# Other slots in the run-out for the gate steps and expert groups of the last three tiles

## The reference, cut to what matters

```python
x = x + 0.5 * ffn(layernorm(x))          # job b
x = x + attention(layernorm(x))          # 16 heads, scores below the 31st largest masked
x = x + 0.5 * ffn(layernorm(x))          # job a

def ffn(h):                              # 16 experts of width 64
    logits = normalize(h) @ normalize(sim) - sigmoid(gates)
    rw = softmax(where(mask, relu(logits), -inf))   # mask: logits > 0, else the top 2
    q, k, v = (sum_e rw[e] * (h @ proj[e]) for proj in (q_proj, k_proj, v_proj))
    att = softmax(causal(q @ k.T / 8)) @ v
    return sum_e (rw[e] * att) @ o_proj[e]
```

## Time and profile before

| | |
|---|---|
| median of 3 runs | 4722.92 us (4720.09 to 4724.39) |
| the profiled execution | 4726.93 us |
| its span in the profile | 4725.1 us |
| mean granted clock of TensorE | 0.933 |
| busy: TensorE, its weight loads | 87%, 72% |
| busy: VectorE, ScalarE, POOL | 93%, 84%, 63% |

### The profile page before, as it was taken

How to read it: one execution, slowest core, us unless ns; L and a number is a source line. 1 busy time by engine, 2 the same in 40 slices (tenths; PEclk the granted TensorE clock), 3 DMA queues, 4 the chain that set the end, 5 groups by cost and what they waited for, 6 DMA issues and landing times. The chain is left out here.

```text
span 4725.1 us, 123794 instructions
## 1 busy us (share of the span) xinstructions
PE 4132.2 (87%) x33100; PEld 3423.4 (72%) x33100; DVE 4393.5 (93%) x10203; ACT 3967.9 (84%) x10181; POOL 2995.0 (63%) x4946
## 2 busy tenths in 40 slices
PE   6778899899999889999998999998899989987777
PEld 5556777777777777777777777777777777765555
DVE  2499999999999999999999999999999999999982
ACT  2488889898898889989888998988899889888772
POOL 1445677677667767766776776677677667654440
PEclk8889999999999999999999999999999999988888
DMA  3111111121111111111111111111111111111011
GB/s 100 45 27 35 49 50 53 50 55 50 52 51 51 53 50 55 50 52 51 51 53 50 55 50 52 51 51 53 50 53 50 54 51 51 51 38 26 22 30 50
DMA packets 244162, 232.66 MB, mean 49 GB/s; under 512 B 27123, under 2 KB 176628, under 8 KB 243316
## 3 DMA queue, kind: packets, MB, share of 16 engines
q1 hardware_dynamic: 243444, 224.49, 16.6%
HBM read 214.98 MB, written 9.44 MB: 47 GB/s over the span
## 5 line engine op out<-in xcount | busy, mean ns | idle before, releaser
L1027 DVE MAX8 M<-W 128x8 f32<-128x512 f32 x2688 | 1735.2, 681 | 57.8 <-DVE W L1029 2.5
L679 PE MATMUL pQ<-wf_sb,HS 128*128 128x192 f32 x8192 | 1545.3, 345 | 81.3 <-POOL HS L419 54.1
L679 PEld LDWEIGHTS pQ<-wf_sb,HS 128*128 128x128 f32 x8192 | 1438.3, 203 | 129.5 <-issue 65.9
L1029 DVE MATCH_REPLACE8 W<-M,W 128x512 f32<-128x512 f32 x1664 | 1115.0, 676 | 0.0
L1072 POOL TENSOR_TENSOR XL<-S,LM 128x512 f32<-128x512 f32 x384 | 445.6, 1160 | 908.4 <-ACT LM L909 895.5
L698 PE MATMUL pST<-ident,S 128*128 128x128 f32 x4096 | 747.9, 283 | 15.4 <-ACT S L897 15.4
L924 ACT ACTIVATE OUT<-S,M 128x512 bf16<-128x512 f32 x1024 | 741.5, 724 | 0.0
L928 ACT ACTIVATE S<-S,M 128x512 f32<-128x512 f32 x1024 | 737.2, 720 | 0.0
L700 PE MATMUL pST<-steep,OUT 128*128 128x128 bf16 x4096 | 731.8, 222 | 0.0
L1029 DVE MATCH_REPLACE8 W<-M,S 128x512 f32<-128x512 f32 x1024 | 684.3, 676 | 0.0
L1027 DVE MAX8 M<-S 128x8 f32<-128x512 f32 x1024 | 651.5, 678 | 20.8 <-ACT S L897 10.7
(11 more groups left out here) (267 smaller groups left out, 6585.2 us busy)
## 6 DMA issues: line engine op xcount, KB each, us to landing
RB<-rows_b SPq DMA_DIRECT2D x384, 256.0 KB, 3.3
RB<-rows_a SPq DMA_DIRECT2D x384, 256.0 KB, 3.3
x_b<-in_x SPq DMA_DIRECT2D x64, 128.0 KB, 2.8
out_y<-y SPq DMA_DIRECT2D x64, 128.0 KB, 1.8
wf_sb<-in_wf SPq DMA_DIRECT2D x4, 768.0 KB, 7.4
rows_b<-rwT_b SPq DMA_DIRECT2D x64, 8.0 KB, 1.3
wof_sb<-in_wof SPq DMA_DIRECT2D x1, 1024.0 KB, 7.1
rows_a<-rwT_a SPq DMA_DIRECT2D x64, 8.0 KB, 1.4
```

The source lines that it names most:

```text
L679: mm = nc.tensor.matmul(pQ[:, 0:QKV], HS[:, k % 2, e, i, :], wf_sb[:, i, at:at + QKV], start=k + e + i == 0, stop=(k, e, i) == (3, 3, 1))
L1027: nc.vector.max(m, src[i]).then_inc(s_tk, 1)
L1029: nc.vector.match_replace(W[:, i, :], m, src[i], -BIG).then_inc(s_tk, 1)
```

## The change

For the last three tiles of job a, a second table `QUICK` gives the gate steps and the four expert groups other slots. Relative to the tile, `shift` to `rw_st` were at slots 50 to 61 and are at 49 to 53, right behind `lg` at 49. `hs` was at 64, 66, 68, 70 and is at 60, 63, 67, 70. The next tile's gate steps, at 65 to 69 on this tile's count, so meet its groups, and its first two groups stand among the small products of the tile before.

The counts of events (`FILLS`, `CHUNKS`) follow the new slots. Three more edits go beyond the last tiles or beside them: `ctx_norm` is no longer moved to VectorE for tiles 62 and 63; `rw_st` waits for the `RB2` load of two tiles before in place of its `mix`, in all tiles; the scaling of `wof` comes 16 slots later in the run-in. `QUICK` has slots for job b too, but its `ENDS` is empty.

```diff
-        "gate_exp": 88, "gate_em": 89, "gate_sum": 90, "rw": 91, "rwT": 92, "rw_st": 93, "hs": 96, "qkv": 104,
+        "gate_exp": 88, "gate_em": 89, "gate_sum": 90, "rw": 91, "rwT": 92, "rw_st": 93, "hs0": 96, "hs1": 98, "hs2": 100, "hs3": 102, "qkv": 104,
...
+ENDS = {"a": range(TILES - 3, TILES), "b": range(0)}
+QUICK = {
+    "a": {k: v - 2 * TILE for k, v in {
+        "shift": 81, "top": 82, "pair": 82, "repl": 83, "gate": 83, "gate_exp": 84, "gate_em": 84, "gate_sum": 85,
+        "rw": 85, "rwT": 85, "rw_st": 85, "hs0": 92, "hs1": 95, "hs2": 99, "hs3": 102}.items()},
...
+def slot_of(n, key, t):
+
+    return (QUICK[n] if t in ENDS[n] and key in QUICK[n] else AT[n])[key] + t * TILE
+
+
+def events(n, key):
+
+    if key not in QUICK[n]:
+        return [(AT[n][key], TILE, TILES)]
+    others = [t for t in range(TILES) if t not in ENDS[n]]
+    return [(slot_of(n, key, others[0]), TILE, len(others))] + [(slot_of(n, key, t), SPAN, 1) for t in ENDS[n]]

...
-CHUNKS = {(n, c): (AT[n]["hs"] + 2 * c, TILE, TILES) for n in "ab" for c in range(4)}
+CHUNKS = [[ev for n in "ab" for ev in events(n, f"hs{k}")] for k in range(4)]
...
-            return due(w, j + ahead, J.at[key], TILE, TILES) if key in J.at else None
+            if key in QUICK[J.n] and w.lo == w.hi:
+                for t in ENDS[J.n]:
+                    if SPAN * w.lo + j + ahead == slot_of(J.n, key, t):
+                        return t, t - TPB * w.lo
+            at = due(w, j + ahead, J.at[key], TILE, TILES) if key in J.at else None
+            return None if at and key in QUICK[J.n] and w.lo == w.hi and at[0] in ENDS[J.n] else at
+
+        def apart(J, t, key, other, back=0):
+
+            if isinstance(t, int):
+                return slot_of(J.n, other, t - back) - slot_of(J.n, key, t)
+            return J.at[other] - J.at[key] - back * TILE
 
         def chunk_no(w, j):
-            return earlier(w, j, CHUNKS.values())
+            return earlier(w, j, sum(CHUNKS, []))
 
...
-            if not isinstance(t, int) or key in ("x_rstd", "h_rinv", "y_rstd"):
+            if not isinstance(t, int) or key in ("x_rstd", "h_rinv", "y_rstd", "ctx_norm"):
                 return False
             if J.n == "b":
                 return t < TPB
-            return t >= TILES - (3 if key in ("hs", "sc_nmax", "sc_rec", "mix") else 2)
+            return t >= TILES - (3 if key[:2] == "hs" or key in ("sc_nmax", "sc_rec", "mix") else 2)
 
...
-                    held(sp, q["read"], fill(J.n, w, j + J.at["rwT"] - J.at["rw_st"]) + 1)
+                    held(sp, q["read"], fill(J.n, w, j + apart(J, t, "rw_st", "rwT")) + 1)
                     if not (isinstance(t, int) and t < 2):
-                        held(sp, s_mix, earlier(w, j + J.at["mix"] - J.at["rw_st"] - 2 * TILE, MIXES.values()) + 1)
+                        held(sp, s_rb2, 32 * earlier(w, j + apart(J, t, "rw_st", "mix", 2), MIXES.values()) + 32)
...
-                    if at := tile(J, "hs", w, j, 3 - 2 * k):
+                    if at := tile(J, f"hs{k}", w, j, 3):
...
-                if (w.lo, j) == divmod(AT["b"]["hs"], SPAN):
+                if (w.lo, j) == divmod(AT["b"]["qkv"] + 8, SPAN):
```

More of the change, by code:

```diff
@@ L67 @@
         "lg": -41, "shift": -40, "top": -39, "pair": -38, "repl": -37, "gate": -34, "gate_exp": -33,
-        "gate_em": -32, "gate_sum": -31, "rw": -30, "rwT": -29, "rw_st": -28, "hs": -24, "qkv": -16, "qkT": -15,
+        "gate_em": -32, "gate_sum": -31, "rw": -30, "rwT": -29, "rw_st": -28, "hs0": -24, "hs1": -22, "hs2": -20, "hs3": -18, "qkv": -16, "qkT": -15,
         "sc": -14, "sc_max": -13, "sc_nmax": -11, "sc_exp": -10, "sc_rec": -9, "sc_norm": -8, "pT": -6,
@@ L72 @@
 }
+ENDS = {"a": range(TILES - 3, TILES), "b": range(0)}
[3 more added lines that the diff above has]
+        "rw": 85, "rwT": 85, "rw_st": 85, "hs0": 92, "hs1": 95, "hs2": 99, "hs3": 102}.items()},
+    "b": {k: v - SPAN for k, v in {
+        "shift": -41, "top": -40, "pair": -40, "repl": -39, "gate": -39, "gate_exp": -38, "gate_em": -38,
+        "gate_sum": -37, "rw": -37, "rwT": -35, "rw_st": -35, "hs0": -30, "hs1": -27, "hs2": -22,
+        "hs3": -19}.items()},
+}
+def slot_of(n, key, t):
[5 more added lines that the diff above has]
+    return [(slot_of(n, key, others[0]), TILE, len(others))] + [(slot_of(n, key, t), SPAN, 1) for t in ENDS[n]]
 PROJ = {"Q0": 57 - SPAN, "K0": 59 - SPAN, "V0": 61 - SPAN, "V1": 62 - SPAN, "Q1": 68 - SPAN, "K1": 70 - SPAN}
@@ L78 @@
 FILLS = {
-    "a": {k: (AT["a"][k], TILE, TILES) for k in ("ctxT", "x", "hT", "lg", "rwT", "qkT", "sc", "pT", "attT", "y")},
-    "b": {k: (AT["b"][k], TILE, TILES) for k in ("hT", "lg", "rwT", "qkT", "sc", "pT", "attT", "y", "xn")}
-    | {k: (s, SPAN, NB) for k, s in PROJ.items()},
+    "a": [ev for k in ("ctxT", "x", "hT", "lg", "rwT", "qkT", "sc", "pT", "attT", "y") for ev in events("a", k)],
+    "b": [ev for k in ("hT", "lg", "rwT", "qkT", "sc", "pT", "attT", "y", "xn") for ev in events("b", k)]
+    + [(s, SPAN, NB) for s in PROJ.values()],
 }
-CHUNKS = {(n, c): (AT[n]["hs"] + 2 * c, TILE, TILES) for n in "ab" for c in range(4)}
+CHUNKS = [[ev for n in "ab" for ev in events(n, f"hs{k}")] for k in range(4)]
 GROUPED = {n: (AT[n]["qkv"], TILE, TILES) for n in "ab"}
@@ L162, in fill @@
 def fill(n, w, j):
-    return earlier(w, j, FILLS[n].values())
+    return earlier(w, j, FILLS[n])
 def build(nc, x, wqk, bqk, wv, bv, wo, bo, sim, gates, wf, wof, out):
@@ L378, in layer @@
                 t, c = at
-                eng.wait_ge(q["read"], fill(J.n, w, j + J.at["lg"] - J.at["shift"]) + 1)
+                eng.wait_ge(q["read"], fill(J.n, w, j + apart(J, t, "shift", "lg")) + 1)
                 ns.tensor_tensor(J.L[:], J.Lr[:], sig[:], ALU.subtract).then_inc(q["shift"], 1)
@@ L410, in layer @@
             for k in range(4):
-                if at := mine("hs", -2 * k):
+                if at := mine(f"hs{k}"):
                     t, c = at
                     m = chunk_no(w, j)
-                    chunks = [ev for key, ev in CHUNKS.items() if key[1] % 2 == k % 2]
+                    chunks = CHUNKS[k % 2] + CHUNKS[k % 2 + 2]
                     eng.wait_ge(s_rb[k % 2], 16 * earlier(w, j, chunks) + 16)
@@ L668, in group @@
                 for k in range(4):
-                    if at := tile(J, "hs", w, j, -1 - 2 * k):
+                    if at := tile(J, f"hs{k}", w, j, -1):
                         t, c = at
@@ L810, in leave @@
                     if not (isinstance(t, int) and t < 2):
-                        act.wait_ge(s_hs, chunk_no(w, j + J.at["hs"] + 6 - J.at["hT"] - 2 * TILE) + 1)
+                        act.wait_ge(s_hs, chunk_no(w, j + apart(J, t, "hT", "hs3", 2)) + 1)
                     act.wait_ge(q["full"], n)
```

## The result

The changed kernel takes 4733.01 us (median of 13 runs, 4731.04 to 4734.31) against 4723.02 (13 runs, 4718.32 to 4724.64) for the kernel before in the same rounds: ratio 1.0021, 95% interval 1.0014 to 1.0028. It is 10 us, 0.2%, slower. The forecast was 4725.5, with 0.72 on a change within 0.2% (9.4 us) and 0.10 on slower; 10.0 us lies just outside those 0.2%, and the time lies on the upper end of the range, where rival C stood.

A forecast was written before the change was run, and what follows sets the result against it. VectorE was taken to set the pace until its last search, so the change could pay only after it, perhaps in the run-in; order +0.1 and clock +2.5 us, +2.6 on the median 4722.92, gave 4725.5 us, range 4711 to 4733.

The forecast's parts named there:

- rival C: Low clock takes group 3 of tiles 60 to 62 and the y matmuls behind: +8.7 to +12, 4731.7 to 4735; chance 0.12.
- The bound: VectorE sets the pace of the middle, so the change can pay only after its last search, perhaps in the run-in.
- Tile 60's stall: HS of tile 60's group 2 waits on POOL behind pair until 4590.4; group 4 ends later, +9.6 us.
- The steps: From group 4 to the next tile's group 1, tiles 60 to 63: gaps shrink by 5.6, 6.7 and 6.8 us.
- The row loads: On SP, gate rows of the next tile return before group 1 needs them, even queued behind the store of y.
- Inside the tiles: Stretches from group 1 to group 4 grow: +3.8 in tile 61, +5.0 in tile 62, +0.8 in tile 63.
- an HS beside it: On VectorE beside POOL's mix: each new overlap with an HS could cost a few tenths through the shared SBUF interfaces.
- The clock: TensorE's lower clock behind stalls before group 3 of tiles 60 to 62, less first groups' gain: +2.5 us.
- the structure's +0.1: Sum of tile 60's stall, the steps and the stretches inside tiles, at the clocks of before: +0.1 us.
- half a first group back: First groups of tiles 62 and 63 may find a high clock, 0 to -5.6; half of one group counted.
- the tail: Work behind tile 63's group 4, 22.1 us long: unchanged.
- The side edits: ctx_norm of tiles 62 and 63 on POOL, later wof scaling, and rw_st's other wait: no gain or cost, 0.

The follow-up runs named there:

- e1: Changed kernel with no tile in the QUICK table, leaving only the three side edits; 4723.81 us, ratio 1.0001 to the kernel before.
- e3: Changed kernel with tile 61's gate steps on VectorE in place of POOL, in the same slots; 4726.14 us, ratio 1.0005 to the kernel before.
- e12: Changed kernel with useless matmuls in the new TensorE holes of tiles 60, 61 and 62; 4726.69 us, ratio 1.0008 to the kernel before.
- e8: Changed kernel with 11 useless matmuls of 512 columns ahead of tile 60's group 2; 4731.15 us, ratio 1.0014 to the kernel before.
- e7: Changed kernel with tile 61's gate steps on VectorE, the last ones later, and groups 3 and 4 of tiles 61 to 63 earlier; 4716.65 us, ratio 0.9987.
- e2: Changed kernel with the quick slots for tiles 62 and 63 only; 4722.53 us, ratio 0.9998 to the kernel before.
- e9: Changed kernel with only tiles 62 and 63 quick, their groups 3 and 4 and some gate steps earlier, rwT and rw_st one slot later; 4715.99 us, ratio 0.9983.
- e10: Kernel before, no slot changed, with useless matmuls ahead of first groups of tiles 61 to 63, two row transposes and tail work; 4716.85 us, ratio 0.9986.
- e11: e9 with useless matmuls ahead of group 1 of tiles 61 to 63 and tile 63's pT and y; 4710.42 us, ratio 0.9974 to the kernel before.

## Why the prediction was right or wrong

**The forecast and the range.** The likeliest value was missed by 7.5 us and the outcome (within 0.2%) by 0.6. That the time stands in the range it owes to rival C, which I gave 0.12.

**The bound, right.** From tile 0's top-8 to tile 61's the profiled executions differ by 0.3 us (4195.6 before, 4195.9 after), and e1 shows nothing of the side edits.

**Tile 60's stall, right.** HS of group 2 ran at 4589.73, behind `pair`, predicted 4590.4. Group 4's end moved by 13.4 us; less what groups 2 and 3 and the product between them lost to the clock (5.49-2.87, 4.28-2.77 and 1.41-1.05, 4.5 in all) that is 8.9, against 9.6. e3 gives the stall of group 2 back by taking tile 61's gate steps out of POOL's queue.

**The steps, right**, each to 0.2 us: -5.4, -6.7, -6.6 against -5.6, -6.7, -6.8. The row loads were in time on SP, also behind `y`.

**Inside the tiles, right but for the clock.** With the clock given back in e12, tile 61 takes 22.2 us and tile 62, with 0.9 us added for its first group's 4.52 in place of before's 5.38, 22.7. Against before's 17.6 and 17.7 that is +4.6 and +5.0, where I had +3.8 and +5.0. Of the 0.8 in tile 61, 0.5 are TensorE's wait for tile 62's `rw`, which is late because `em_a` takes 2.33 us beside POOL's mix; I had priced an HS beside it, at a few tenths, but not the gate steps.

**The clock, wrong: this is the step that failed.** I put it at +2.5: "+1.9 for two of the three, and half a first group back". Measured against the structure's +0.1, it is 7.8 - 0.1 = +7.7. Three things are behind it. I gave two of the groups 3 the loss of tile 61's first group, 1.9, where groups 3 of tiles 61 and 62 took 5.33 and 5.49 against 2.77, a loss of 2.6 and 2.7; the first groups of tiles 62 and 63, 5.38 and 5.46, stood in the same rows, and the range had them as its upper bound. All three groups 3 lost, not two. And tile 60's group 2, behind the longest hole of all (11.25 us idle), was not in the clock's term or in rival C: 5.49, a loss of 2.6, and 0.4 in the product behind it. The four groups and that product lost 9.8 us by their rows, or 8.9 as they delay what follows (tile 61's loss of 2.6 delayed it by only 1.7; in e12 TensorE waits 0.5 us for `rw` there). First groups gave back 0.2 in tile 62 and some 0.4 in tile 63, not the 1.3 that were in the +2.5, and the tail 0.6. Rival C, with a chance of 0.12, had the right cause and nearly the size (7.7 for its 8.7 to 12), but not the right places: it was four groups rather than three, and the y products behind groups 3 ran at the full clock (1.89 to 1.99 us each, as before); only the product behind tile 60's group 2 was slow.

The Trainium skill (TensorE: Matmul & The Clock Gate, HAM oscillation) has the engine start the next burst at the lower clock after a long wait between bursts. The trace agrees behind the hole of 11.25 us, with 0.50 granted. It shows the same behind short waits, 0.53 behind 2.38 us and 0.50 behind 1.94, and 0.64 over tile 60's group 3 (4.28 us).

**The side edits, right:** `ctx_norm`, `wof` and `rw_st` at 0 (e1). In the changed kernel and in e1 `wof`'s scaling comes later and its wait is gone.

**What stays open.** Where the low clock falls next when one hole is filled (e8, e12) was seen, not foreseen: in step 60 to 61 the same work ran at either level behind the same 1.99 us of idle TensorE. How much a group pays is open too: the wait ahead of tile 62's first group is 2.31 us in ten of the kernels, and the group behind it took 4.32 (e7) to 5.46 us (e2). So a row of one execution prices a hole only to about a microsecond, and the split of the 7.7 over the places holds for the profiled execution alone. The median moved by 10.0 us, the run-out of the profiled executions by 7.8. Whether the other 2.2 lie in the first 400 us, where the profiled executions differ most, or in longer run-outs of those that were not profiled, no run here tells.

## What to carry to other kernels

When a step is moved ahead in one tile, look up which queue it enters and what stands behind it: a gain of 18.7 us in three gaps was spent by one early copy on POOL and two HS behind a gate chain on VectorE, and the same rows ahead, for two tiles, gained 9.5 us of run-out once nothing waited behind them (e9). Price every new hole on TensorE together with the group behind it, as a range that reaches up to the slowest such group of the trace, and count every hole. Useless matmuls in a short hole can be worth their place at the end of a program (e10, e11), but they must fit the hole, at the lower clock if they can meet it (e11; e12's was too long even at the full one), and only a run tells whether the low stretch is gone or has moved.

## What the runs showed of the hardware

- VectorE's small instructions stretch beside a long one of POOL. In the changed kernel `em_a`, with two inputs, beside POOL's mix in tile 61's stretch (first two rows), and alone in tile 62's (last row):

```profile
4640.25 2.79 POOL L476 TENSOR_TENSOR mixT<-attT_a,RB 128x1024 f32<-128x1024 f32 x1 [6.46 <-ACT attT_a L883]
4640.77 2.32 DVE L442 TENSOR_TENSOR em_a<-eg_a,mk_a 128x16 f32<-128x16 f32 x1
...
4673.84 0.17 DVE L442 TENSOR_TENSOR em_a<-eg_a,mk_a 128x16 f32<-128x16 f32 x1
```

It also struck a product with one tensor and a column of factors (`rw_a` in e7, 1.50 in place of 0.23). The Trainium skill (GPSIMD Engine Reference, section 1, Specifications) has the two engines contend for their shared SBUF interfaces when VectorE's instruction has two SBUF inputs or runs in a 2-port performance mode. The trace agrees for `em_a`; whether `rw_a` ran in such a mode, no run here shows. The trace adds the size: the short instruction ends with POOL's long one (4643.09 and 4643.04 here), however little it has to do. The HS that VectorE had begun 0.6 us before the mix kept its usual 1.23 us; there the mix was the longer one, 2.79 in place of 2.36.
- A group of 16 at the full clock takes 2.8 us and at the low one 5.3 to 5.5, the latter already behind 1.94 us of idle TensorE (4673.97, granted 0.50). The length of the wait does not settle it: behind the same 2.31 us the first group of tile 62 took 4.32 us in e7 (granted 0.65), 5.18 in the changed kernel and 5.46 in e2 (0.50). Yet in the changed kernel the 1.99 us ahead of the attention's output product cost nothing (1.13 us), while in e12 it took 1.79.
- Filled holes can pass the low stretch on: e8 gained 2.6 us in one group, lost 1.1 in the next and 3.1 in the step behind, and ended 0.2 us ahead.
